# Four shared result blocks in a row, between the shared rows of the small products, in a fused normalisation and channel attention

## What is computed

```python
x = x + _L0_conv_ref(_gn(x), w_qkv, temperature, w_out, b_out)
# _gn: 32 groups of 6 channels, mean and variance per image
# _L0_conv_ref:
qkv = xt @ w_qkv                                  # xt: (b, 2304, 192)
q = q / max(sqrt(sum(q * q over n)), EPS)         # k alike, then * temperature
attn = softmax(einsum('bhpn,bhnq->bhpq', k, q))   # 24 x 24 for each head
out = einsum('bhnp,bhpq->bhnq', v, attn) @ w_out + b_out
```

## Time and profile before

| | us |
|---|---|
| median of 3 runs | 374.44 (373.13 to 374.47) |
| the profiled execution | 374.76 |
| its span, first to last instruction | 372.8 |
| TensorE busy in the span | 331.2 (89%) |
| VectorE busy | 283.2 (76%) |
| ScalarE busy | 235.9 (63%) |
| GpSimd busy | 150.4 (40%) |

### The profile page before, as it was taken

How to read it: one execution, slowest core, us unless ns; L and a number is a source line. 1 busy time by engine, 2 the same in 40 slices (tenths; PEclk the granted TensorE clock), 3 DMA queues, 4 the chain that set the end, 5 groups by cost and what they waited for, 6 DMA issues and landing times.

```text
span 372.8 us, 9327 instructions
## 1 busy us (share of the span) xinstructions
PE 331.2 (89%) x3724; PEld 233.4 (63%) x3724; DVE 283.2 (76%) x666; ACT 235.9 (63%) x410; POOL 150.4 (40%) x133
## 2 busy tenths in 40 slices
PE   0048856999999999999999999999999999999795
PEld 0036645875778566865777577856686577765452
DVE  4889855887699669986799769966998665359774
ACT  1098489763997299747996399729974699610200
POOL 0079858301970169203950197016920395001000
PEclk9999976899999999999999999999999999999999
DMA  7999900004994279815991499427981563034766
GB/s 235 359 286 246 244 16 3 2 2 139 300 323 132 86 233 326 247 44 137 336 335 44 134 297 338 124 87 226 320 261 45 165 217 88 2 105 150 230 213 192
DMA packets 30826, 67.73 MB, mean 182 GB/s; under 512 B 5504, under 2 KB 12096, under 8 KB 30784
## 3 DMA queue, kind: packets, MB, share of 16 engines
q1 hardware_dynamic: 30544, 66.56, 56.7%
q10 hardware_dynamic: 240, 0.59, 0.6%
HBM read 29.38 MB, written 28.31 MB: 155 GB/s over the span
## 4 chain that ended last, share of the span: by engine, by line
PE 64%; ACT 15%; issue 10%; DVE 5%; DMA 2%; SPq 2%; POOL 1%; ACTq 0%; POOLq 0%
PE u_ps L927 30%; PE g_ps L927 17%; PE s_ps L927 10%; ACT h_sb L543 4%; ACT tok L581 4%; ACT xn L537 3%; PE u_ps L976 2%; DMA wo<-in_L_conv_w_out_dram 2%; PE u_ps L977 2%; ACT h_sb L550 1%; DVE x_sb L855 1%; PE u_ps L979 1%; PE u_ps L978 1%; SPq L354 1%; SPq L359 1%
## 5 line engine op out<-in xcount | busy, mean ns | idle before, releaser
L474 POOL TENSOR_TENSOR l_sb<-xn,h_sb 128x768 f16<-128x768 f32 x63 | 103.8, 1649 | 56.0 <-ACT h_sb L543 55.7
L855 DVE SCALAR_TENSOR_TENSOR x_sb<-u_ps,bias,x_sb 128x384 f32<-128x384 f32 x144 | 85.9, 613 | 24.2 <-PE u_ps L927 24.1
L927 PE MATMUL g_ps<-tok 128*128 128x64 f16 (+1 forms) x864 | 87.1, 241 | 3.4 <-ACT tok L581 2.9
L537 ACT ACTIVATE xn<-x_sb,rb 128x768 f32<-128x768 f32 x63 | 63.6, 1020 | 29.7 <-POOL rb L486 29.7
L581 ACT COPY tok<-u_ps 128x384 f32<-128x384 f32 x144 | 65.0, 485 | 19.8 <-PE u_ps L979 18.6
L927 PEld LDWEIGHTS g_ps<-tok 128*128 128x128 f16 x864 | 57.0, 99 | 28.5 <-ACT tok L581 5.8
L728 DVE BATCH_NORM_STATS2 bnst<-x_sb 128x6 f32<-128x384 f32 x144 | 69.9, 543 | 5.3 <-DMA x_sb<-in_x_dram 5.2
L927 PE MATMUL u_ps<-h_sb,ml 128*128 128x384 f16 (+1 forms) x336 | 73.2, 327 | 0.0
L543 ACT ACTIVATE h_sb<-x_sb,rb 128x768 f16<-128x768 f32 x63 | 64.4, 1022 | 0.0
L976 PE MATMUL u_ps<-id,h_sb 128*128 128x128 f16 x288 | 48.9, 223 | 8.2 <-DVE l_sb L718 7.4
L977 PE MATMUL u_ps<-id,l_sb 128*128 128x128 f16 x288 | 48.9, 223 | 0.0
(11 more groups left out here) (144 smaller groups left out, 567.6 us busy)
## 6 DMA issues: line engine op xcount, KB each, us to landing
x_sb<-in_x_dram SPq DMA_DIRECT2D x48, 384.0 KB, 5.4
out_dram<-x_sb SPq DMA_DIRECT2D x48, 384.0 KB, 2.9
out_dram<-x_sb SPq DMA_DIRECT2D x48, 192.0 KB, 2.8
x_sb<-in_x_dram SPq DMA_DIRECT2D x45, 192.0 KB, 5.4
hl<-h_sb SPq DMA_DIRECT2D x48, 96.0 KB, 2.8
hl<-l_sb SPq DMA_DIRECT2D x48, 96.0 KB, 3.0
x_sb<-in_x_dram ACTq DMA_DIRECT2D x3, 192.0 KB, 4.2
w<-in_L_conv_w_qkv_dram SPq DMA_DIRECT2D x1, 288.0 KB, 7.4
```

Of the source, the lines that this page charges most:

```text
L474: nc.gpsimd.tensor_tensor(l_sb[:, par, t, cols], xn[:, c % XN_RING, :], h_sb[:, par, t, cols], ALU.subtract).then_inc(l_ok, 1)
L537: nc.scalar.activation(xn[:, c % XN_RING, :], xcol(q, t, g * GW, GW), ACT.Identity, bias=rb[:, par, 1, t:t + 1], scale=rb[:, par, 0, t:t + ...
L855: V.scalar_tensor_tensor(out=xs, in0=block_ps(n), scalar=bias[:, t:t + 1], in1=xs, op0=ALU.add, op1=ALU.add).then_inc(out_ok, 1)
L927: return nc.tensor.matmul(dst, lhs, rhs, start=start, stop=stop, skip_group_check=True)
```

## The change

- *Order of the result blocks.* In group 1 the shared tile comes first: n6 and n7 are now shared blocks, n8 to n11 are full ones. With n4 and n5, four shared blocks stand in a row. n16 and n17 stay.
- *Parts of the shared blocks.* n4 makes its lower-weights matmul, waits for n5's bank and, with `sums`, for the reduction of the group sums (which n5 waited for before), and makes n5's lower-weights matmul; then comes w0 (`"in 4"`), then the halves of n4. n5 is its halves. n6 and n7 make their halves; then comes w1 (`"in 7"`), then the lower-weights matmuls of both. n16 and n17 have theirs first and last, as before.
- *w1* makes its shared rows first and the whole rows after them; t_mm counts t2 first (`T_AT`). w0 keeps its order.
- *ScalarE and VectorE* take t2 ahead of t0 and t1. VectorE copies z behind n3 (was n4), takes t2 behind n5 and t0, t1 behind n7 (all three were behind n6).
- *SyncE* stores and loads in the new order, with a semaphore for stores for each tile and group; the copies of halves come behind the third chunk of a group.

No matmul, copy or transfer is added or removed.

```diff
@@ -67,21 +67,21 @@
-PE_B = {0: ["gram"], 2: ["sums"], 4: ["w0"], 6: ["w1"], 12: ["scores"]}
+PE_B = {0: ["gram"], 2: ["sums"], "in 4": ["w0"], "in 7": ["w1"], 12: ["scores"]}
...
-ACT_B = ["x0", "t0", "t1", "t2", "h0", 1, 2, 3, 4, 5, "x6", "x7"]
+ACT_B = ["x0", "t2", "t0", "t1", "h0", 1, 2, 3, 4, 5, "x6", "x7"]
...
-VEC_B = {0: ["gram"], 2: ["var"], 4: ["z"], 6: ["t0", "t1", "t2"], 12: ["norms"], 17: ["spread", "bn", "bn", "bn", "bn"]}
+VEC_B = {0: ["gram"], 2: ["var"], 3: ["z"], 5: ["t2"], 7: ["t0", "t1"], 12: ["norms"], 17: ["spread", "bn", "bn", "bn", "bn"]}
...
-FIRST_ACT_B = [0, "x1", "t0", "t1", "t2", "h1", 2, 3, 4, 5, "x6", "x7"]
+FIRST_ACT_B = [0, "x1", "t2", "t0", "t1", "h1", 2, 3, 4, 5, "x6", "x7"]
...
-FIRST_VEC_B = {0: ["gram", "var", "z", "t0", "t1"], 1: ["t2", "bn", "bn", "wo", "norms", "spread", "bn", "bn"]}
+FIRST_VEC_B = {0: ["gram", "var", "z", "t2", "t0"], 1: ["t1", "bn", "bn", "wo", "norms", "spread", "bn", "bn"]}
@@ -91,10 +91,10 @@
-LAST_ACT_B = ["t0", "t1", "t2", "exp", "v"]
+LAST_ACT_B = ["t2", "t0", "t1", "exp", "v"]
...
-LAST_VEC_B = {0: ["gram"], 2: ["z"], 3: ["t0", "t1", "t2"], 5: ["norms"], 8: ["spread"], 10: ["soft_in"], 12: ["soft_out"],
+LAST_VEC_B = {0: ["gram"], 2: ["z"], 3: ["t2", "t0", "t1"], 5: ["norms"], 8: ["spread"], 10: ["soft_in"], 12: ["soft_out"],
@@ -112,7 +112,8 @@
-    OUTS = [(t, g * GW + k * BW) for g in range(GROUPS) for t in (0, 2, 1) for k in (0, 1)]
+    ROWS = [(t, g) for g in range(GROUPS) for t in ((1, 0, 2) if g == 1 else (0, 2, 1))]
+    OUTS = [(t, g * GW + k * BW) for t, g in ROWS for k in (0, 1)]
@@ -232,7 +233,7 @@
-        stored = [sem(f"stored{t}") for t in range(3)]
+        stored = [[sem(f"stored{t}_{g}") for g in range(GROUPS)] for t in range(3)]
@@ -294,6 +295,8 @@
+        T_AT = (2, 3, 1)
@@ -371,23 +374,23 @@
-                landed = [fixed((p * GROUPS + g + 1) * (32 if t == 1 else 16)) for t, g in CHUNKS]
+                landed = [fixed((p + 1) * (32 if t == 1 else 16)) for t, g in ROWS]
...
-                        t, g = CHUNKS[k]
+                        t, g = ROWS[k]
...
-                            sp.dma_start(dram, chip).then_inc(stored[t], 16)
-                        if t == 1 and not (isinstance(p, int) and p + 1 == PAIRS):
+                            sp.dma_start(dram, chip).then_inc(stored[t][g], 16)
+                        if k % 3 == 2 and not (isinstance(p, int) and p + 1 == PAIRS):
...
-                        t, g = CHUNKS[k - LOAD_LAG]
-                        sp.wait_ge(stored[t], landed[k - LOAD_LAG])
+                        t, g = ROWS[k - LOAD_LAG]
+                        sp.wait_ge(stored[t][g], landed[k - LOAD_LAG])
@@ -424,8 +427,8 @@
-            for t in range(3):
-                sp.wait_ge(stored[t], PAIRS * GROUPS * (32 if t == 1 else 16))
+            for t, g in ROWS:
+                sp.wait_ge(stored[t][g], PAIRS * (32 if t == 1 else 16))
@@ -622,7 +625,7 @@
-                act.wait_ge(t_mm, 3 * q + k + 1)
+                act.wait_ge(t_mm, 3 * q + T_AT[k])
@@ -844,7 +847,7 @@
-                dve.wait_ge(th_ok, 3 * q + k + 1)
+                dve.wait_ge(th_ok, 3 * q + T_AT[k])
@@ -1029,28 +1032,37 @@
                 else:
                     pe.wait_ge(z_ok, q + 1)
-                for b in (0, 1):
-                    dst = g_ps[:, b, 0:2 * C]
-                    hi, lo = (q16[:, b, i, 0:P] for i in (0, 1))
+                def whole_rows():
+                    for b in (0, 1):
+                        dst = g_ps[:, b, 0:2 * C]
+                        hi, lo = (q16[:, b, i, 0:P] for i in (0, 1))
+                        if not ready:
+                            mm(dst, hi, wh0[:, :], True)
+                            mm(dst, hi, wl0[:, :], False)
+                            mm(dst, lo, wh0[:, :], False)
+                        else:
+                            mm(dst, z[:, b, 0:P], wh1[:, :], False)
+                            mm(dst, z[:, b, 0:P], wl1[:, :], False, True).then_inc(t_mm, 1)
+                def shared_rows():
                     if not ready:
-                        mm(dst, hi, wh0[:, :], True)
-                        mm(dst, hi, wl0[:, :], False)
-                        mm(dst, lo, wh0[:, :], False)
-                    else:
-                        mm(dst, z[:, b, 0:P], wh1[:, :], False)
-                        mm(dst, z[:, b, 0:P], wl1[:, :], False, True).then_inc(t_mm, 1)
-                if not ready:
-                    need(pe, ml_ok, 2 * q)
-                for k in (range(3, 5) if ready else range(3)):
-                    for b in (0, 1):
-                        dst = s_ps[C1 * b:C1 * b + C1, 0, 0:2 * C]
-                        hi, lo = (q16[:, b, i, P:C] for i in (0, 1))
-                        lhs, rhs = ((hi, wh0), (hi, wl0), (lo, wh0), (z[:, b, P:C], wh1), (z[:, b, P:C], wl1))[k]
-                        last = mm(dst, lhs, rhs[:, :], k == 0, k == 4)
+                        need(pe, ml_ok, 2 * q)
+                    for k in (range(3, 5) if ready else range(3)):
+                        for b in (0, 1):
+                            dst = s_ps[C1 * b:C1 * b + C1, 0, 0:2 * C]
+                            hi, lo = (q16[:, b, i, P:C] for i in (0, 1))
+                            lhs, rhs = ((hi, wh0), (hi, wl0), (lo, wh0), (z[:, b, P:C], wh1), (z[:, b, P:C], wl1))[k]
+                            last = mm(dst, lhs, rhs[:, :], k == 0, k == 4)
+                    if ready:
+                        last.then_inc(t_mm, 1)
                 if ready:
-                    last.then_inc(t_mm, 1)
+                    shared_rows()
+                    whole_rows()
                     return
+                whole_rows()
+                shared_rows()
                 if q == 0:
                     pe.wait_ge(gstep, GVAR + 1)
@@ -1122,46 +1134,69 @@
                                       wo[:, j, P * b:P * b + C], j == 0 and k == 0, j == 1 and k == 2)
                 last.then_inc(m_mm, 1)
-            def result(q, par, n, sums):
+            def result(q, par, n, sums, between):
                 (t, c), w = OUTS[n], BW
+                h, l = (a[:, par, :, :] for a in (h_sb, l_sb))
+                def bank_free(n):
+                    if n >= RING:
+                        pe.wait_ge(out_ok, (q + 1) * NO + n - RING + 1)
+                    elif isinstance(q, int) and q == PAIRS - 1:
+                        pe.wait_ge(out_ok, q * NO + NO - RING + (n + SLOTS) % RING + 1)
+                def lower_weights(n, start):
+                    at = OUTS[n][1]
+                    return mm(block_ps(n), ml1[:, 1, :], h[:, 1, at:at + w], start, not start)
+                def two_halves(start):
+                    dst = block_ps(n)
+                    for b in (0, 1):
+                        mm(dst[C1 * b:C1 * b + C1, :], mh1[:, b, P - P * b:C - P * b], hl[:, b, c:c + w], start)
+                    for k, (m, a) in enumerate(((mh0, h), (mh0, l), (ml0, h))):
+                        for b in (0, 1):
+                            last = mm(dst[C1 * b:C1 * b + C1, :], m[:, b, P:C], a[:, 2 * b, c:c + w], False,
+                                      k == 2 and not start)
+                    return last
                 if n == 0:
                     pe.wait_ge(ml_ok, 2 * q + 2)
                     pe.wait_ge(mh_ok, 3 * q + 3)
-                if n >= RING:
-                    pe.wait_ge(out_ok, (q + 1) * NO + n - RING + 1)
-                elif isinstance(q, int) and q == PAIRS - 1:
-                    pe.wait_ge(out_ok, q * NO + NO - RING + (n + SLOTS) % RING + 1)
-                if sums:
-                    pe.wait_ge(gstep, (q + 2) * GVAR + 1)
+                if n not in (5, 17):
+                    bank_free(n)
                 if n % (NO // GROUPS) == 0:
                     pe.wait_ge(hl_in[n // (NO // GROUPS)], (q + 1) * 64)
-                dst = block_ps(n)
-                h, l = (a[:, par, :, c:c + w] for a in (h_sb, l_sb))
                 if t != 1:
-                    b = t // 2
-                    mm(dst, mh0[:, b, 0:P], h[:, t, :], True)
-                    mm(dst, mh0[:, b, 0:P], l[:, t, :], False)
-                    mm(dst, mh1[:, b, C1 * b:C1 * b + P], hl[:, b, c:c + w], False)
-                    mm(dst, ml0[:, b, 0:P], h[:, t, :], False)
-                    mm(dst, ml1[:, t, :], h[:, 1, :], False, True).then_inc(out_mm, 1)
+                    b, dst, x = t // 2, block_ps(n), slice(c, c + w)
+                    mm(dst, mh0[:, b, 0:P], h[:, t, x], True)
+                    mm(dst, mh0[:, b, 0:P], l[:, t, x], False)
+                    mm(dst, mh1[:, b, C1 * b:C1 * b + P], hl[:, b, x], False)
+                    mm(dst, ml0[:, b, 0:P], h[:, t, x], False)
+                    mm(dst, ml1[:, t, :], h[:, 1, x], False, True).then_inc(out_mm, 1)
+                elif n in (4, 16):
+                    lower_weights(n, True)
+                    bank_free(n + 1)
+                    if sums:
```

(38 more changed lines are left out.)

## The result

| | before | after |
|---|---|---|
| median, us | 374.00 (12 runs, 372.62 to 374.68) | 378.11 (12 runs, 375.24 to 379.72) |
| ratio, 95% interval | | 1.0121 (1.0101 to 1.0141) |
| span of the profiled run, us | 372.8 | 376.7 |
| start of n0 in step 0 | 80.96 | 78.72 |
| six periods, n0 of step 0 to n0 of step 6 | 242.68 | 246.30 |

The change makes the kernel 1.2% slower; 0.7% faster was forecast. The first stretch differs from kernel to kernel: n0 of step 0 starts at 77.3 to 81.0 us in the fourteen profiled kernels, at a mean granted clock up to it of 0.91 to 0.98 that does not follow its length. So I compare by the two lower lines: 3.6 us more in the six periods (40.95 us each for most, 40.45 before) and 2.5 us more at the end.

A forecast was written before the change was run, and what follows sets the result against it. ScalarE was taken as almost the bound up to the first token copies and TensorE behind it; 6 x 0.41 + 0.23 = 2.7 us off the profiled 374.76 or median 374.44 gave 371.8 us, range 369.8 to 373.9.

The forecast's parts named there:

- What bounds the kernel: From the copies of t to about 151.6 us ScalarE is almost the bound, its only pause 0.46 us; behind it TensorE.
- Fewer passages: TensorE leaves full-array work three times a period instead of six, saving 0.66 us a period on its own path.
- The new order laid on the old clock: Result blocks to first token copy: h0 starts 0.14 us later, at 132.25; 0.41 us a period is won.
- VectorE: Evictions and copies of t in the new order: at least 0.45 us in hand for TensorE's banks, nothing lost.
- The moved wait: n5's lower matmul now waits for the group variance's first reduction: cost zero, cover 0.2 us.
- The ends: First step and step 6 gain nothing; step 7 saves one passage, 0.23 us.
- the slower one: Rival: the reduction holds back n5's lower matmul, 0.16 us longer a period, 375.2 us in all; chance 0.06.
- Rival C: Evictions bind: VectorE a microsecond late, TensorE stands 0.55 us at n12, total 0.9 us less; chance 0.05.
- Rival A: TensorE alone decides, ScalarE's pause and start do not matter: 4.2 us less; chance 0.14.
- rival E: Passages are not saved: gaps fall at bank changes, between n5, n6 and n7, and the time stays; chance 0.07.
- The sum: Six periods at 0.41 us plus 0.23 us in step 7: 2.7 us less over the whole kernel.

The follow-up runs named there:

- e3: The changed kernel with n17's wait moved back ahead of n17 and the clamp reading PSUM; ratio 0.9971 to the kernel before.
- e6: e3 with ScalarE's passes moved: x7 behind token copy 2, h7 to 4, x8 to 7, h8 to 9; ratio 0.9987 to the kernel before.
- e8: The kernel before with only ScalarE's passes moved as in e6; ratio 1.0060 to the kernel before.
- e1: The changed kernel with the wait for n17's bank moved back from n16 to n17; ratio 1.0011 to the kernel before.
- e2: The kernel before with only the wait for n17's bank moved early, ahead of n16's halves; ratio 1.0117 to the kernel before.
- e4: The changed kernel with only the clamp reading PSUM, the early wait for n17's bank kept; ratio 1.0042 to the kernel before.
- e5: e3 with SyncE storing and loading the chunks in the old order; ratio 0.9960 to the kernel before.
- e9: e6 with ScalarE's pass x8 back at place 5 and h8 at 7; ratio 1.0001 to the kernel before.
- e10: e9 with SyncE's old order of stores and loads; ratio 0.9996 to the kernel before.
- e11: The kernel before with the clamp reading PSUM and ScalarE's passes placed as in e9; ratio 1.0058 to the kernel before.
- e7: e5 and e6 together: SyncE's old order and ScalarE's passes moved; ratio 0.9951 to the kernel before.
- e12: e10 with ScalarE's pass h8 at place 8 rather than 7; ratio 0.9976 to the kernel before.

## Why the prediction was wrong

**What bounds the kernel:** right. ScalarE's run of passes had 0.46 us of pause; the 8.72 us of e3 against the 8.41 of e6, with nothing gained there in e8, show that this run is the limit once TensorE gains more.

**Fewer passages, 0.66 a period:** right, 0.68 measured from n0 to the scores.

**The new order laid on the old clock:** right up to the scores. n5's lower matmul did not wait. ScalarE's h0 started at 130.56, which on the old clock (1.73 later) is 132.29; 132.25 was forecast.

**VectorE:** here it failed, first. The step followed VectorE to the scores (n8's bank for n12) and said "nothing lost". It stopped before n13 to n17, where VectorE has the norms between n12 and n13, and it took each duration as fixed. The clamp's 0.21 us in the old trace already held a little waiting (0.16 in e3). When TensorE and so the norms moved 0.68 us forward, while GpSimd's pass, which follows ScalarE's run, moved 0.19 back, the same instruction grew by 0.85 to 1.06. The gain never reached the evictions of n13 and later.

**The moved wait:** here it failed, second. I followed the wait for the sums at n5 and did not list the other wait that the same branch moves, n17's bank at n16. By my own rule, each wait with what is queued behind it, it was there in the diff: n4 and n16 share the branch. e1 and e2 put its price at 0.65 us a period in the new order and 0.33 in the old, and at 1.2 us and more at the end. In the periods it costs only where n13's eviction is late: beside the short clamp of e4 it costs nothing. Over the whole kernel it weighs more than the clamp: moved back alone it takes the ratio from 1.0121 to 1.0011, the clamp alone to 1.0042.

**The ends:** step 6 was set at nothing, and it cost 1.2 us for the late attention step. Together with the half clock that followed in step 7, it is the 2.5 us of the first table. The half clock is no part of the mechanism: it came or stayed away at the same waits (last section). Step 7's one passage was worth about 0.2, as forecast: its end is 49.0 in e5, e6, e9 and e10 and 49.2 in the kernel before, e8 and e11.

**The rivals:** the slower one was put on the wrong wait and at a fifth of the real price (0.8 of 4.1 us). Rival C was the nearest in kind (evictions bind), though its place (n12) was wrong. Rival A is excluded by the 8.72 of e3, rival E by the half pairs without a gap.

**The sum:** with both failures mended (e3, e5) the period of 40.07 gives the forecast 0.4. The whole comes to 0.3% to 0.4% less instead of 0.7%, since late loads take back 0.2 us of it a period on average (241.5 and 241.9 against 6 x 40.07 = 240.4).

## What to carry to other kernels

When a branch is shared by two places of a loop, list the waits of each place, the one the change is not about too, and lay every queue out to the end of the loop and not to the first point where it looks safe. If one engine is moved forward and its neighbours are not, a small instruction that ends together with a neighbour's long one may already be waiting for it, and its duration will grow by all that is gained.

## What the runs showed of the hardware

- A VectorE tensor_scalar of 96x8 float32 with its operand and result in SBUF took 1.06 us beside a GpSimd tensor_tensor and ended with it (140.68 and 140.67, 140.22 and 140.19); with the operand in PSUM it took 0.16 us in the middle of such a pass. The profile shows the wait as part of the instruction's duration (0.21 or 1.06 us), not as idle time before it.
- A passage between full-array and 64-column matmuls costs about 0.22 us there and back, while a change of bank among half pairs costs nothing: sixteen pairs in four banks ran at 0.16 us each.
- TensorE's granted clock was 0.50 to 0.56 for the first 3 us of step 7 in five of fourteen profiled kernels (after, e1, e3, e7, e12), after waits of 1.0, 0.3 and 1.5 us (or 2.3 and 1.5), and 1.00 in the nine others after the same waits. In two of these nine, e2 and e4, it had been 0.50 and 0.78 in step 6, for 3 us behind the wait of 2.3 us. It makes the end 1.4 to 1.7 us longer, over half of the 2.7 us that the change was to bring. What decides it is not shown.
